# One transformer block on one core: maxima rows sent early, part of the first group's attention moved into the prologue, and narrow masked scores of both head pairs in one bank

## The reference

```
Q, K, V = x @ qw, x @ kw, x @ vw          # heads of 8
Q, K = rope(Q, freq), rope(K, freq)
score = einsum(Q, K) / sqrt(8) - 1e10 * (1 - causal)
weights = softmax(score - max(score))     # over keys
x = layernorm(x + merged(weights @ V) @ ow)
gates = top-2 of softmax(x @ router_w + router_b), renormalised
h = silu(x @ w1[e]) * (x @ w3[e])
x = layernorm(x + sum_e gates[e] * (h @ w2[e]))
```

## Time and profile before

| | |
|---|---|
| median of three runs | 449.56 us (447.17 to 450.29) |
| the profiled execution | 448.0 us, of which the span (first to last instruction) is 446.0 us |
| up to the first score on DVE | 25.5 us |
| prologue, from there to its join | 34.2 us |
| first stage with attention, join to join | 39.75 us |
| each of the six stages after it, join to join | 26.55 us |
| last join to the first expert matmul | 26.35 us |
| experts to the end | 160.9 us |
| mean granted TensorE clock | 0.945 of 2.4 GHz |

### The profile page before, as it was taken

The page is one execution under the profiler, slowest core; times in us unless marked ns, Lnnn a source line. Parts: engine busy times, 40 slices in busy tenths (PEclk is TensorE's granted clock), DMA queues, the critical chain, the costliest instruction groups (busy, mean ns, idle before and its releaser), DMA issues.

```text
span 446.0 us, 7534 instructions
## 1 busy us (share of the span) xinstructions
PE 398.0 (89%) x2420; PEld 205.1 (46%) x2420; DVE 313.5 (70%) x1027; ACT 265.6 (60%) x377; POOL 193.7 (43%) x256
## 2 busy tenths in 40 slices
PE   4667626999999999999999988899999999999991
PEld 1352102323232322323333232488887888788780
DVE  3549934999898989989999854236567658656743
ACT  1232204677677767777776778675655666665560
POOL 6625502125143442424335140365546646655661
PEclk9959655999999999999999998999999999999996
DMA  6472651131221313221130000000000000000000
GB/s 214 151 203 82 216 122 40 24 89 34 67 48 35 80 23 79 46 68 38 30 85 13 1 3 1 1 0 2 0 2 24 1 1 0 25 1 3 24 0 24
DMA packets 45244, 21.13 MB, mean 47 GB/s; under 512 B 30995, under 2 KB 42899, under 8 KB 45206
## 3 DMA queue, kind: packets, MB, share of 16 engines
q1 hardware_dynamic: 44950, 20.47, 17.6%
q10 hardware_dynamic: 256, 0.20, 0.2%
HBM read 13.11 MB, written 7.35 MB: 46 GB/s over the span
## 4 chain that ended last, share of the span: by engine, by line
PE 69%; DVE 14%; issue 7%; ACT 4%; POOL 3%; DMA 1%; ACTq 0%; POOLq 0%; SPq 0%; DVEq 0%
PE o_bank L1097 14%; PE bank L1057 10%; PE t_bank L1165 9%; PE t_bank L1176 8%; PE bank L1165 8%; PE t_bank L1080 7%; PE small_bank L1057 5%; DVE maxima L828 4%; DVE mg_w L824 2%; DVE mg_t L824 2%; DVE num L885 1%; DVE x_w L824 1%; ACT num L669 1%; DVE num L958 1%; PE t_bank L1015 1%
## 5 line engine op out<-in xcount | busy, mean ns | idle before, releaser
L669 ACT ACTIVATE num<-t_bank 128x1024 f32<-128x1024 f32 (+2 forms) x160 | 142.5, 938 | 74.6 <-PE t_bank L1080 74.1
L583 POOL TENSOR_TENSOR hid_lo<-num,q_op 128x512 fp32r<-128x512 f32 x64 | 83.1, 1301 | 60.8 <-ACT q_op L723 59.7
L547 POOL TENSOR_SCALAR_AFFINE_SELECT num<-num 128x512 f32<-128x512 f32 x64 | 39.9, 638 | 109.6 <-ACT num L669 108.3
L1057 PE MATMUL bank<-k_op,q_op 128*128 128x512 bf16 (+7 forms) x258 | 77.4, 337 | 10.3 <-DMA k_op<-k_scratch 6.8
L1097 PE MATMUL o_bank<-num,v_op 128*32 128x512 f32 (+3 forms) x768 | 81.5, 503 | 0.1
L723 ACT ACTIVATE q_op<-num 128x512 fp32r<-128x512 f32 x64 | 40.5, 632 | 45.1 <-DVE num L958 44.7
L1080 PE MATMUL t_bank<-q_op,k_op 64*128 64x512 bf16 (+3 forms) x384 | 52.6, 338 | 12.9 <-issue 11.5
L828 DVE TENSOR_REDUCE maxima<-bank 128x1 f32<-128x512 f32 x86 | 59.0, 686 | 3.1 <-PE bank L1057 3.1
L1057 PEld LDWEIGHTS bank<-k_op,q_op 128*128 128x128 bf16 x258 | 22.8, 98 | 67.5 <-DVE maxima L824 32.0
L824 DVE CUSTOM_DVE_ANT_0 mg_t<-bank,resid 128x320 f32<-128x320 f32 (+6 forms) x87 | 39.0, 448 | 18.1 <-PE small_bank L1057 11.5
L1057 PE MATMUL small_bank<-k_op,q_op 128*128 128x512 bf16 (+7 forms) x126 | 42.2, 335 | 3.1 <-DVE maxima L828 2.7
(11 more groups left out here) (133 smaller groups left out, 646.1 us busy)
## 6 DMA issues: line engine op xcount, KB each, us to landing
q_op<-q_scratch SPq DMA_DIRECT2D x64, 48.0 KB
w_raw<-in_w_all SPq DMA_DIRECT2D x6, 512.0 KB, 4.2
k_op<-k_scratch SPq DMA_DIRECT2D x60, 48.0 KB, 1.9
q_scratch<-num SPq DMA_DIRECT2D x4, 384.0 KB, 2.7
k_scratch<-num SPq DMA_DIRECT2D x4, 384.0 KB, 2.6
xT<-in_x_feat SPq DMA_DIRECT2D x4, 256.0 KB, 5.7
q_scratch<-num SPq DMA_DIRECT2D x4, 256.0 KB, 2.1
k_scratch<-num SPq DMA_DIRECT2D x4, 256.0 KB, 2.6
```

The lines of the kernel that those rows point to most:

```text
L547: pool.affine_select(out=tile, in_=tile, compare_op=ALU.is_ge, fill=0.0, base=0, pattern=[[0, GH], [1, P]], channel_multiplier=-1)\
L583: pool.tensor_tensor(hid_lo[:, m % HB, :], hid[:, m % HB, :], hid_hi[:, m % HB, :].bitcast(F32), ALU.subtract).then_inc(f_lo, 1)
L669: act.activation(num[:, t % PB, :, off:CH].rearrange("p (k i) t -> p i k t", i=2)[:, :, h:h + each, :], t_bank[k % TB][:, :, 0:each * (CH ...
L1057: pe.matmul(ring(s, step)[:, 0:width], q_op[u][:, pr, j, :, :].rearrange("p i q -> p (i q)"), k_op[u][:, pr, lo:lo + width], start=True, s ...
```

## The change

- **Rows early.** SP loads group 1 and sends the rows of the prologue's MROWS before the last four stores. The parts of those four projections move out of `num` into `x_res` and `w_raw`, which are loaded later, so that ACT need wait only for the first four stores.
- **Part of group 0 in the prologue.** The T and PV steps of the first half of group 0's queries run in the prologue (`T_AT`, `PV_AT`), between its S steps, with its OCOPY. The first stage after it, `FIRST`, is the steady order without them: four T steps and four PV steps fewer. `ahead` in a PV or OCOPY step says that it belongs to the stage's own group.
- **Pairs share a bank.** Where the scores of both pairs of a query block fit in 512 columns together (width up to 256), they are one job: two matmuls side by side, one signal; two masked reduces, one signal. A group has 40 jobs for the same 48 matmuls and 48 reduces.
- **Order.** `STEADY_ORDER` is written anew for 40 jobs; MROWS of the previous group comes after two jobs (four matmuls), both NORMs lie behind the last S. P comes at jobs 12 to 20. `rden` gets a buffer for each half.

```
-S_UNITS = [(j // NB, pr, j, half) for j in range(S // QB) for pr in range(NPR) for half in range(j // NB + 1)]
+S_UNITS = [(j // NB, prs, j, half) for j in range(S // QB) for half in range(j // NB + 1)
+           for prs in (((0, 1),) if NPR * s_width(j, half) <= CH else ((0,), (1,)))]
...
-PROJ_AT = (16, 20, 24, 28, 32)
+PROJ_AT = (12, 14, 16, 18, 20)
+T_AT, PV_AT = (22, 24, 25, 27, 28, 30), (29, 31, 33, 35)
...
+            if done_s in T_AT:
+                plan.append(("T", *T_UNITS[T_AT.index(done_s)], 1))
+            if done_s in PV_AT:
+                plan.append(("PV", 0, PV_AT.index(done_s), 1))
             plan.append(("S", *unit))
             done_s += 1
-            if done_s == SEG_S[0] + 5:
+            if done_s == SEG_S[0] + 3:
                 plan.append(("MROWS", 0))
+        return [(*step, 0) if step[0] == "MROWS" else step for step in plan + [("OCOPY", 0, 1), ("END",)]]
...
-STEADY_ORDER = ("ssstssstsmstsntsspssspssttspsspsstsstsspsmsttsspsssttnsspttssspssttsspssttsspstsstpp")
+STEADY_ORDER = "ssmttssspssttsspssttsspsstspsttssspmsttsssptsspssttssspssttsspssttsspsnttnpp"
...
+FIRST = steady_plan(STEADY_ORDER.replace("t", "", SEG_T[0] - T_END[0]).replace("p", "", TI), done=TI - 1)
-STAGES = [PROLOGUE] + [STEADY] * (GROUPS - 1) + [LAST]
+STAGES = [PROLOGUE, FIRST] + [STEADY] * (GROUPS - 2) + [LAST]
...
+        late = [x_res[:, :, :].rearrange("p i d -> p (i d)").bitcast(BF16).rearrange("p (n t) -> p n t", t=CH),
+                w_raw[:, :].bitcast(BF16).rearrange("p (n t) -> p n t", t=CH)]
+
+        def rope_part(n, r):
+
+            if n < 2 * NC:
+                return early[:, n, r, :]
+            k = (n - 2 * NC) * PARTS + r
+            return late[k // 8][:, k % 8, :]
...
-            for n in range(2 * NC, 2 * CHUNKS):
-                store(n)
             sp.wait_ge(ops_filled, 4)
             for c in range(NC):
                 load_q(sp, 1, 1, c, range(GH))
                 load_k(sp, 1, 1, c)
+
+            def send_rows(s, step, to):
+                c = step[1]
+                sp.wait_ge(job_read, SB + JOB[s, step] + 1)
+                for h in range(GH):
+                    sp.dma_start(
+                        q_op[to][h % 2 * HR + KROWS:h % 2 * HR + QROWS, h // 2, c * NB:(c + 1) * NB, h % 2, :],
+                        max_rows[c][h // 2 * PARTS * NB:(h // 2 + 1) * PARTS * NB, h % 2 * QB:(h % 2 + 1) * QB])\
+                        .then_inc(rows_loaded[c], 16)
+
+            send_rows(0, next(step for step in PROLOGUE if step[0] == "MROWS"), 0)
+            for n in range(2 * NC, 2 * CHUNKS):
+                store(n)
...
-            for ch in range(CHUNKS):
+            for ch in range(NC):
                 act.wait_ge(parts_stored[ch], 2 * PARTS * 16)
...
-                        pe.matmul(ring(s, step)[:, 0:width], q_op[u][:, pr, j, :, :].rearrange("p i q -> p (i q)"),
-                                  k_op[u][:, pr, lo:lo + width], start=True, stop=True).then_inc(job_ready, 1)
+                        for i, pr in enumerate(prs):
+                            ins = pe.matmul(ring(s, step)[:, i * width:(i + 1) * width],
+                                            q_op[u][:, pr, j, :, :].rearrange("p i q -> p (i q)"),
+                                            k_op[u][:, pr, lo:lo + width], start=True, stop=True)
+                        ins.then_inc(job_ready, 1)
```

More of the change, by code:

```diff
@@ L92, in stage_plan @@
     t_units = [(u, 0) for u in T_UNITS[T_END[0]:]] if with_t else []
-    t_units += [(u, 1) for u in T_UNITS[:T_END[0]]] if with_s else []
     def s_work(units):
-        return sum(60 + min(CH, QB * (j + 1) - half * CH) for _, _, j, half in units)
+        return sum(60 + len(prs) * s_width(j, half) for _, prs, j, half in units)
     def t_work(units):
@@ L287, in transformer_block @@
         o_sb = [sb(f"o_sb{c}", [P, CH]) for c in range(NC)]
-        rden = sb("rden", [P, TI, GH])
+        rden = sb("rden", [P, NC, TI, GH])
         merged = sb("merged", [P, GROUPS + 1, S // P, QD])
@@ L452, in stage @@
                         load_k(sp, s + 1, v, 1)
-            for s, plan in enumerate(STAGES):
-                stage(plan, s, s % 2, load=0 < s < GROUPS - 1)
+            for s in range(1, GROUPS + 1):
+                stage(STAGES[s], s, s % 2, load=s < GROUPS - 1)
             for ch in range(0, CHUNKS):
@@ L531, in stage @@
                             third_part(step[1] - 1)
-                    if plan is STEADY and step == ("T", 1, 1, 0, 0):
+                    if 0 <= n < GROUPS - 1 and step == ("T", 1, 1, 0, 0):
                         pool.wait_ge(pv_done, PB + NPV * n)
@@ L568, in _ @@
             for n in range(GROUPS - 1):
-                stage(STEADY, n, 1 - n % 2, split=n > 0)
+                stage(STAGES[n + 1], n, 1 - n % 2, split=n > 0)
             def between(ch, r, first=False):
@@ L673, in stage @@
                     if step[0] == "OCOPY":
-                        c = step[1]
-                        act.wait_ge(pv_done, PB + NPV * n + (TI if c == 0 else NPV))
+                        _, c, ahead = step
+                        act.wait_ge(pv_done, PB + NPV * (n + ahead) + (TI if c == 0 else NPV))
                         act.wait_ge(job_ready, last_norm(n + 1, c))
@@ L680, in stage @@
                         between(0, 0, 0, step[1], first=True)
-            stage(PROLOGUE, -1)
-            for n in range(GROUPS - 1):
-                stage(STEADY, n, split=n > 0)
+            for n in range(-1, GROUPS - 1):
+                stage(STAGES[n + 1], n, split=n > 0)
             def between(ch, b, c, r, first=False):
@@ L811, in stage @@
                     if step[0] == "S":
-                        _, c, pr, j, half = step
-                        k = S_UNITS.index((c, pr, j, half))
-                        lo = half * CH
-                        width = min(CH, QB * (j + 1) - lo)
+                        _, c, prs, j, half = step
+                        width = s_width(j, half)
                         if s > 0 and c not in seen:
@@ L820, in stage @@
                         dve.wait_ge(job_ready, job + 1)
-                        if QB * (j + 1) - lo <= CH:
-                            if k == 0 and plan is PROLOGUE:
-                                dve.wait_ge(ld_small, 16 * 2)
-                            dve.tensor_tensor_reduce(masked_s[job % SB][:, 0:width], ring(s, step)[:, 0:width],
-                                                     causal[:, CH - width:CH], 1.0, LOWEST, ALU.add, ALU.max,
-                                                     maxima[:, half, pr, j:j + 1]).then_inc(job_read, 1)
-                        else:
-                            dve.tensor_reduce(maxima[:, half, pr, j:j + 1], ring(s, step)[:, 0:width], AX.X, ALU.max)\
-                                .then_inc(job_read, 1)
+                        for i, pr in enumerate(prs):
+                            at = slice(i * width, (i + 1) * width)
+                            if half == c:
+                                if j == 0 and i == 0 and plan is PROLOGUE:
+                                    dve.wait_ge(ld_small, 16 * 2)
+                                ins = dve.tensor_tensor_reduce(
+                                    masked_s[job % SB][:, at], ring(s, step)[:, at], causal[:, CH - width:CH],
+                                    1.0, LOWEST, ALU.add, ALU.max, maxima[:, half, pr, j:j + 1])
+                            else:
+                                ins = dve.tensor_reduce(maxima[:, half, pr, j:j + 1], ring(s, step)[:, at],
+                                                        AX.X, ALU.max)
+                        ins.then_inc(job_read, 1)
                         done += 1
@@ L1035, in _, with stage @@
             pe.sem_inc(pv_done, PB)
-            def stage(plan, s, u, turn_u, turn_v):
+            def stage(plan, s, u, turn_u):
                 n = s - 1
@@ L1121, in stage @@
                         between(0, step[1] - 1, first=True)
-            stage(PROLOGUE, 0, 0, 1, 0)
-            pe.wait_ge(ops_filled, 6)
-            for s in range(1, GROUPS):
-                stage(STEADY, s, s % 2, s // 2 + 1, (s + 1) // 2)
+            for s in range(GROUPS):
+                stage(STAGES[s], s, s % 2, s // 2 + 1)
+                if s == 0:
+                    pe.wait_ge(ops_filled, 6)
             def between(ch, r, first=False):
@@ L1190, in _ @@
             pe.wait_ge(ld_small, 16 * 6)
-            stage(LAST, GROUPS, 0, 0, GROUPS // 2)
+            stage(LAST, GROUPS, 0, 0)
             pe.wait_ge(c_top, 2)
```

64 lines of the change are left out of this document (30 added, 34 removed).

## The result

The changed kernel takes 433.87 us in the median of four runs (432.75 to 435.27), the kernel before beside it 449.93 (four runs): a ratio of 0.9666, 95% interval 0.9628 to 0.9703, or 16 us less. The profiled execution took 432.75 us, its span is 430.7; that is 15.3 less than the span of before (446.0). The span is cut at the joins (DVE's `TENSOR_TENSOR maxima<-maxima`) as before.

A forecast was written before the change was run, and what follows sets the result against it. The prediction took PE to bound the steady stages by a little, DVE 2.35 us behind. Its terms: 448.0 + 1.0 - 12.95 - 5.1 + 0.4 = 431.4, toward the median of runs 432; range 424 to 440.

The forecast's parts named there:

- Rows early: Prologue: rows go out in SP's free 7.3 us, land at 46.5, T about 49.5; the wait on PE costs nothing.
- One sign by which the prediction was to be called wrong: In the prologue: the prediction is wrong if PE stands before T there; no size given.
- Prologue: Prologue with T and PV in it: DVE's work stays 29.8 us, clock falls near 48; +1.0 us (-1 to +5).
- First stage: First stage with attention: the stall goes, DVE becomes the bound; 26.8 us (25.3 to 29) for 39.75, so -12.95.
- Steady stages: Six equal stages: fewer changes of matmul kind save PE time; 25.7 us each for 26.55, 6 x -0.85 = -5.1.
- MROWS just fits: Steady join: split ready 3.3 us after the last S matmul, PE has 3.25 us of work between.
- A rule against the pairing: Paired jobs: DVE's reduce starts only when both matmuls are done; at most 1.2 us a stage, taken as nothing.
- Last stage: At its start: NORM and PV left over on PE, ACT's ahead exponentials some 1.5 us later; +0.4 (0 to 1.5).
- The stages don't shrink: Rival, steady stages: DVE starves at the join as much as PE gains, 26.55 stays; 436.5 us, chance 0.22.
- DVE's floor: Rival, steady stages: the order brings both engines to 24.6 us each, prologue gains 1 us; 423 us, chance 0.14.
- the slow prologue: Rival, prologue: stays at half clock, PE the bound from T on, +5 instead of +1; 437.5 us, chance 0.12.
- rows that don't leave early: Rival, prologue: sends wait for the last stores, T stands 8 us with S queued behind; 439.4 us, chance 0.04.

The follow-up runs named there:

- e1: The kernel before with only the rows sent early and the late parts in x_res and w_raw: 435.90 us, ratio 0.9707.
- e3: The changed kernel with the prologue's rows sent behind the last four stores again: 440.04 us, ratio 0.9819 to the kernel before.
- e8: The changed kernel with some score matmuls of prologue and first stage repeated into the same bank to hold the clock up: 432.38 us, ratio 0.9625.
- e6: The changed kernel with the first stage's MROWS two jobs later: 434.48 us, first stage 26.27 us.
- e2: The changed kernel with nothing of group 0 in the prologue but two T at its end, and seven equal stages: 433.51 us, ratio 0.9644.
- e4: The changed kernel with every paired job split in two again, PE's matmul order kept: 449.42 us, ratio 1.0007 to the kernel before.
- e5: The changed kernel with the old steady order adapted to 40 paired jobs; its first stage changed too: 438.69 us, ratio 0.9777.
- e9: The changed kernel with the pairs of query blocks 0 to 3 undone, PE's order kept: 438.93 us, ratio 0.9775.
- e10: The changed kernel with the pairs of query blocks 8 to 11 undone, PE's order kept: 444.83 us, ratio 0.9915.
- e7: The changed kernel with two S jobs and a PV moved ahead of the steady stage's first T on the new rows: 437.69 us, ratio 0.9761.
- e11: e2 with score matmuls repeated as in e8, in the prologue and the first two jobs of the first stage: 431.44 us, ratio 0.9615.
- e12: e11 with the prologue's P steps at jobs 12, 15, 18, 21 and 24: 431.75 us, ratio 0.9622.

## Why the prediction was right, and where it was not

**Rows early: right.** The rows left from 40.67 (predicted 40.5), the last stores were issued by 52.5 (54 to 55), `x_res` was issued by 58.8 (60), and the next rows were wanted at 62.86 (62 to 63). T started at 47.41 against 49.5. One sign by which the prediction was to be called wrong did come: PE stood before T, for 1.74 us. The prediction had looked at the landing of the rows and not at ACT, whose last split of the projections T waits for. It cost DVE little (0.26 us of idle time at 48.6). e1 and e3 show that this alone is the greater part: 11.2 us on the first stage.

**Prologue: +0.81 against +1.0, with the parts off.** The six units before the first V took DVE's early idle time from 4.29 to 2.57 us, a gain of 1.7 where I had up to 1. Behind 36.09 DVE stands 24.38 - 22.21 = 2.17 us, against 0.12 before, and its own work, taken as unchanged, is 30.27 us for 29.79. That the sum comes within 0.2 us of the forecast is luck, with a spread of 1.4 us in this place. The clock fell at 44, not near 48, and rose 6 us later, as assumed; in e8's comparison that is worth 0.86 us.

**First stage: -13.54 against -12.95.** Its two waits were as predicted: 1.17 us at MROWS (1.2) and 0.88 behind T (1.0). DVE's own work was the term that was off: 23.22 us where I had put the 24.3 of a full stage. The new order puts both NORMs behind the last S, so behind the join; their two reciprocals and two products on DVE, 1.1 us, are missing between the first two joins and turn up after the last one. e6 shows that the two waits are one: the rows' path from the join to T is the limit, and moving MROWS only moves the wait. The slow clock from 61 to 71 us, not predicted here, costs another 0.62 (e8).

**Moving T and PV: no term went wrong, but one was missing.** The prediction priced what the move adds to the prologue and takes from the first stage, and never the kernel without it. e2 has 1.82 us less of prologue for 0.81 more of first stage, and the sign of it is DVE's idle time behind 36.09: 22.56 - 21.84 = 0.72 us there, 2.17 with T and PV in the prologue. As said, part of the difference of the joins may be chance.

**Steady stages: the size right, -0.71 each against -0.85, its cause only half.** The step that failed is "what pairing saves is on PE: each change from one kind of matmul to another costs about 0.09 us", with pairs themselves worth nothing: under the new order they are worth 2.1 us a stage (e4), and what they change is what the ring of three holds. Four kernels and the two halves, one steady stage each:

| | runs of equal letters | jobs, longest run of S | stage | PE busy | PE idle | DVE idle |
|---|---|---|---|---|---|---|
| before | 54 | 48, 3 | 26.55 | 26.42 | 0.13 | 2.35 |
| e5: pairs, old order | 53 | 40, 3 | 26.65 | 26.25 | 0.40 | 2.52 |
| e4: no pairs, new order | 46 | 48, 5 | 27.95 | 25.98, short of records | 1.97, of it 1.50 waiting | 3.46 |
| e9: pairs of blocks 8 to 11 | 46 | 44, 5 | 26.65 | 25.98 | 0.67 | 2.39 |
| e10: pairs of blocks 0 to 3 | 46 | 44, 4 | 27.13 | 26.11 | 1.02 | 2.70 |
| after: both | 46 | 40, 3 | 25.82 | 25.60 | 0.22 | 1.64 |

With pairs, fewer changes of kind do lower PE's busy time, 26.25 to 25.60, 0.093 us for each of seven, which is the price that the prediction used. Without pairs the same is not to be seen. e4's trace lacks three score matmuls in each stage, and so does the trace of e1, whose steady stage is that of before to the last instruction:

```profile
114.54:141.09 26.55, 25.97 (x201) 8.32 (x203) 24.19 (x87) 19.59 (x24) 9.84 (x20) 1.00 0.23 52
```

It reads 25.97 us busy (x201) where before has 26.42 (x204). With these 0.45 us put back, e4's PE is busy 26.43, as much as before, and stands for 1.5 us and not 1.97. Part of a wait shows as busy time, too: a matmul that starts behind a wait counts with its whole 0.39 us, one that follows another adds 0.23.

The coarser order puts up to five unpaired S jobs in a row before a ring of three banks. PE then stands for DVE to free one, and T and PV, queued behind, stand too; all that the order saved is lost, and 1.4 us more. With pairs the same matmuls are at most three jobs in a row, and the idle time is 0.22. Each edit alone gains nothing (+1.40, +0.11); together they gain 0.71. That the ring is the limit is read from the waits and from where e9 and e10 lose their time; a ring of four was not tried. The length of the runs alone doesn't give the loss: e10, with four in a row, loses more than e9 with five.

**MROWS just fits: right, and one step further.** It starts 1.75 us behind the join without a wait on PE. What comes next is the landing of the rows, which I had called only in the first stage: the chain now runs through it, 7.0 us from join to T, of which the landing behind the last issue is 1.82 us. The Trainium skill (DMA: Bandwidth & Descriptors, Latency and other measured facts) puts a transfer's fixed cost at about 2 us; the 1.82 us agree. e7 shows that later T is no way out.

**A rule against the pairing:** no run isolates the wait for both matmuls. DVE's idle time fell from 2.35 to 1.64 us a stage, but with the same work in a shorter stage it had to. The nearest bound is e5 against before, where pairs came in and the order stayed about the same: DVE idle 2.52 for 2.35, stage +0.11. So it costs little, if anything.

**Last stage: +1.35 against +0.4, the reason right and its size too small.** The prediction said that ACT's two ahead exponentials come some 1.5 us later against the join, and took only 0.4 of that. Rows of ACT, before (join at 258.71) and after (241.72):

```profile
262.19 1.03 ACT L669 ACTIVATE num<-t_bank 128x1024 f32<-128x1024 f32 x1
265.36 1.51 ACT L669 ACTIVATE num<-t_bank 128x512 f32<-128x512 f32 x2 [2.14 <-PE t_bank L1080]
```
```profile
246.57 1.02 ACT L696 ACTIVATE num<-t_bank 128x1024 f32<-128x1024 f32 x1
249.73 1.51 ACT L696 ACTIVATE num<-t_bank 128x512 f32<-128x512 f32 x2 [2.14 <-PE t_bank L1109]
```

The first lies 3.48 us behind the join before and 4.85 after, the second 6.65 and 8.01: the whole difference is there within 5 us of the join, and nothing behind makes it good. The clock is not the reason, since it falls once in both, 16 to 17 us behind the join.

The clock does account for the differences among the new kernels. In this stage it falls to 1.2 GHz for 3 to 4 us, in some executions once, in some twice, in some not at all. With the new order the stage takes 26.4 us without such a fall (e4, e8), 27.5 to 27.7 with one some 17 us behind the join (after, e3, e6, e7, e11), and 29.2 with two (e2, e9, e10, e12). The old order took 26.35 with one (before; e1 26.17, with its one early) and 27.76 with two (e5), so at an equal number of falls the new order is 1.2 to 1.5 us longer. What decides how many there are stays open; e2's and e12's profiled times carry some 1.5 us more of it than the time of after.

**The rivals.** "The stages don't shrink" needed 26.55 and was wrong as a whole, though e4 is its mechanism (fewer changes of kind, and DVE idle 3.46 us a stage where it was 2.35); "DVE's floor" (24.6) was not reached, since PE stays the bound; the slow prologue and rows that don't leave early did not come; and the clock is 1.00 at every steady join.

## What to carry to other kernels

A small transfer that something waits for belongs in the queue at the moment when its data are ready; look there before any rearrangement of the compute engines, as here it was most of the gain (e1 alone brings 2.9%, everything together 3.3%). Test edits that share a reason both alone and together: a coarser order and larger jobs in the ring were each worth nothing or less, and 0.7 us a stage as a pair. Look at a ring's depth in jobs, and at how many of its jobs follow one another in the order. Before you compare busy times of two traces, compare the counts beside them: three missing records looked like 0.45 us saved. And, once a stage is tight, look for the path from its last maximum to the first work that needs it.

## What the runs showed of the hardware that was not expected

- The granted clock can fall in the last stage while PE is mostly busy; after, it stood at 0.50 from 259 to 262 us, with PE busy 4.9 of the 6 us ahead of it, and each such fall went with a stage longer by 1.1 to 1.7 us (26.4, 27.5 to 27.7, 29.2 us).
- Half clock cost little where DVE set the pace: some 16 us of it in prologue and first stage cost about 0.86 + 0.62 us (e8), the first of the two within the spread of equal prologues. In e10's first stage 13 us of it went with 29.23 us, where after has 26.21 and e4, with 3 us of it, 26.52; that is not explained.
- Matmuls that repeat a score into the same bank held the clock at 1.00 from 38 to 88 us in e8, with DVE's busy time unchanged (23.22 and 23.13 in the first stage). In e11, with fewer repeats behind the join, it fell at 61.7 us all the same.
